# Layer 0 of a gated graph network: the gate's bias as a VectorE add in PSUM in place of a matrix product of ones with its rows

## The chip, the cores and the metric

The kernel runs on one core of one Trainium2 chip. The time is the device time of one execution in microseconds (us), the median of the runs shown. A core has TensorE (PE in the rows; PEld is its loading of weights, the stationary operand, which overlaps the products), VectorE (DVE), ScalarE (ACT), GpSimd (POOL) and the queue that issues the transfers (SP). Each engine works through its own instructions in order and waits for others by semaphores.

## The reference, cut to what matters

The input `x` is 128 graphs of 128 nodes with 256 features, `adj` one 128x128 matrix for each graph. Layer 0 is

```
norm  = (sum(adj, -1) + 1e-6) ** -0.5
f_hom = (adj @ ((x @ theta) * norm)) * norm
f_het = x @ W_h
gate  = sigmoid(x @ W_t + b_t)
x     = layernorm(x + elu(gate * f_hom + (1 - gate) * f_het))
```

Layer 1 (a convolution along the nodes, done by way of spectra, a message product and a gated recurrent cell) follows on the result. The change concerns only how `b_t` gets into `gate`.

## The kernel before

The program has four phases, one after the other: `phase_a` (layer 0, and beside it the spectra of layer 1's filter taps), `phase_spectrum`, `phase_product` and `phase_c`. The change touches `phase_a` alone.

**The tiles.** `phase_a` takes two graphs at a time: 64 pairs. Every product is done at nearly full precision by splitting both operands into a high and a low part (`xh`, `xl`, `w_hi`, `w_lo`) and adding three products (low by high, high by low, high by high), for each of the two halves of the 256 features. So `x @ [theta, W_h]` is 6 products of 512 columns for each graph, into `ps_hh` (line 594), and `x @ W_t` 6 products of 256 columns for each graph, 12 for the pair, into the one PSUM bank `ps_g` (line 640). Ahead of these 12 stands one more product, of a 128x128 tile of ones with `bt_rows` (line 637, 512 columns), which puts the bias in all rows of both halves of `ps_g`. In `bt_rows` row 0 holds the high part of the bias, row 1 the low part, and the others are zero; ScalarE and VectorE make it once, in `more_constants` (lines 302 and 448 to 452).

**The order.** It is written by hand. A step `i` of `step` issues on every engine one stage of several pairs at once: `live(s)` says whether pair `i - s` exists. All 64 + 8 steps are written out, with no loop at run time, and a step looks alike on each engine (numbers are lines):

- TensorE: degrees (603, 604), `x @ [theta, W_h]` of graph 0 (594), fourth spectrum product (586), `adj @ f` of the pair before (615), first spectrum product, 594 of graph 1, second spectrum product, transposes of a finished pair (631), the gate (637, 640), third spectrum product.
- ScalarE: `below` and `ex`, the two halves of elu (342, 345), copy of the fourth spectrum (324), `xh` (353), `ah` (355), `fh` of graph 0 (316), copy of the first spectrum, in every fourth step `th` (366), `fh` of graph 1 (316), `het` (370), copy of the second, `x1t` (377), tanh of the gate, in place in `ps_g` (380), copy of the third spectrum.
- VectorE: `sums_eps` of the degrees (504), `y` (508), statistics (512, 517), `diff` (524), `gd` (531), `mix` (534), `fl` of both graphs (540), `x1` (547), `sums_eps` of the variances (553), in every fourth step `tl` (558).

The four spectrum products of a step go through one PSUM bank, `ps_w`: each waits (`s_gw`) until ScalarE has copied the one before it out. That couples the two queues four times in a step. The gate's products may start when VectorE has read the old `ps_g` (`s_gd`); the tanh waits until they are done (`s_gp`):

```
if live(2):
    reached(act, s_gp, p2 + 1)
    nc.scalar.activation(ps_g[:, :, :], ps_g[:, :, :], ACT.Tanh, scale=0.5).then_inc(s_gate, 1)
if ahead(6):
    spectra_out(t - 6, 2)
```

`sigmoid(z)` is used as `0.5 * (tanh(z / 2) + 1)`; `gd` and `mix` apply the rest.

Of the kernel before, what the change touches and what calls it, by code (L numbers as in the profile page):

```python
# [7 lines left out]
F32 = mybir.dt.float32  # L8
F32R = mybir.dt.float32r
ALU = mybir.AluOpType  # L10
ACT = mybir.ActivationFunctionType

P = 128
D = 256
# [16 lines left out]
def reached(eng, sem, count):  # L31

    if isinstance(count, int) and count <= 0:
        return
    eng.wait_ge(sem, count)
# [34 lines left out]
def phase_a(nc, G, x_n, x_t, adj_t, w0, b_t, masks, x1_t, taps, taps_s, dft_w, w_spec, w_c1, bn1, dft_f, keep, s_spec, s_out, first_x, s_x):  # L70
# [16 lines left out]
    with ExitStack() as ctx:  # L87
        def sb(name, shape, dt=F32):
            return ctx.enter_context(nc.sbuf_tensor("a_" + name, shape, dt))

        def sem(name):
            return ctx.enter_context(nc.semaphore("a_" + name))
# [5 lines left out]
        w_hi = sb("w_hi", [P, KD, 3 * D], F32R)  # L98
        w_lo = sb("w_lo", [P, KD, 3 * D], F32R)
        bt_raw = sb("bt_raw", [P, D])  # L100
        bt_hr = sb("bt_hr", [P, D], F32R)
        bt_h = sb("bt_h", [P, D])
        bt_l = sb("bt_l", [P, D])
        bt_rows = sb("bt_rows", [P, 2, D], F32R)
        ones0 = sb("ones0", [P, P])
        ones = sb("ones", [P, P], F32R)
        ident = sb("ident", [P, P])
        mk = sb("mk", [P, 5])
# [54 lines left out]
        ps_g = ctx.enter_context(nc.psum_tensor("a_ps_g", [P, 2, D], F32))  # L163
# [17 lines left out]
        s_root = sem("norm_and_rstd")  # L181
        s_proj = sem("projected")
        s_gp = sem("gate_projected")
        s_fl = sem("f_low")
        s_het = sem("het_copied")
        s_gate = sem("gate_ready")
# [106 lines left out]
        def _(act):  # L293
# [5 lines left out]

            def more_constants():  # L300
                nc.scalar.activation(dw_hi[:, :], dw_raw[:, :], ACT.Copy).then_inc(s_wh, 1)
                nc.scalar.activation(bt_hr[:, :], bt_raw[:, :], ACT.Copy).then_inc(s_wh, 1)

            def step(i, n, k, live):
                u = n % 2
# [70 lines left out]
                    reached(act, s_out[v], (p - v) * 8)  # L376
                    nc.scalar.activation(x1t[:, v], ps_t[:, :, :], ACT.Copy).then_inc(s_x1t, 1)
                if live(2):
                    reached(act, s_gp, p2 + 1)
                    nc.scalar.activation(ps_g[:, :, :], ps_g[:, :, :], ACT.Tanh, scale=0.5).then_inc(s_gate, 1)  # L380
                if ahead(6):
                    spectra_out(t - 6, 2)
# [54 lines left out]
        def _(dve):  # L437
# [3 lines left out]
                nc.vector.tensor_tensor(w_lo[:, :, :], w_raw[:, :, :], w_hi[:, :, :].bitcast(F32), ALU.subtract).then_inc(s_wl, 1)  # L441

            def more_constants():
                dve.wait_ge(s_wh, 4)

                nc.vector.scalar_tensor_tensor(dw[:, :], dw_hi[:, :].bitcast(F32), mk[0:ROWS, 3:4], dw_raw[:, :],
                                               ALU.mult, ALU.add).then_inc(s_wl, 1)
                nc.vector.tensor_tensor(bt_l[:, :], bt_raw[:, :], bt_hr[:, :].bitcast(F32), ALU.subtract).then_inc(s_wl, 1)
                nc.vector.tensor_scalar(bt_h[:, :], bt_hr[:, :].bitcast(F32), mk[:, 0:1], None, ALU.mult).then_inc(s_wl, 1)
                dve.wait_ge(s_wl, 4)  # L450
                for b in range(2):
                    nc.vector.scalar_tensor_tensor(bt_rows[:, b], bt_l[:, :], mk[:, 1:2], bt_h[:, :], ALU.mult, ALU.add).then_inc(s_wl, 1)

            def step(i, n, k, live):
                u = n % 2
# [93 lines left out]
                if live(5):  # L549
                    reached(dve, s_mv, p5 + 1)  # L550

                    reached(dve, s_root, p5 + 3)
                    nc.vector.scalar_tensor_tensor(sums_eps[:, v, 2:4], mv[:, v, :, 1], 1.0, eps[:, :], ALU.mult, ALU.add).then_inc(s_ve, 1)
                if ahead(1) and tn % TB == 1:
                    m = t // TB
                    reached(dve, s_th, m + 1)
                    reached(dve, s_ts, 48 * m)
                    nc.vector.tensor_tensor(tl[:, :], tr[:, :], th[:, :].bitcast(F32), ALU.subtract).then_inc(s_tl, 1)
# [3 lines left out]
        @block.tensor  # L562
        def _(pe):
            pe.wait_ge(s_wl, 1)
            pe.wait_ge(s_wh, 2)
            pe.wait_ge(s_k, 5)

            def step(i, n, k, live):
                u = n % 2
                v = 1 - u  # L570
                t, tn, tk = i + LEAD, (i + LEAD) % UNROLL, (i + LEAD) // UNROLL
                ahead = taps_live(i)
                p2 = i - 2
                terms = [(xx, ww, c) for c in range(KD) for xx, ww in ((xl, w_hi), (xh, w_lo), (xh, w_hi))]

                def spectra(q, c):
                    r = q % RING
                    if c == 0:
                        reached(pe, s_gs[r], 16 * (q // RING + 1))
                    if q == 0 and c == 0:  # L580
                        pe.wait_ge(s_wl, 2)
                    if t == 18 + LEAD and c == 3:

                        pe.wait_ge(s_ch, 1)
                    reached(pe, s_gw, 4 * q + c)
                    nc.tensor.matmul(ps_w[:, 0:GW], gs[:, r, c], dw[:, :], start=True, stop=True).then_inc(s_gm, 1)  # L586

                def project(b):
                    if b == 0:
                        reached(pe, s_xl, p2 + 1)  # L590
                        reached(pe, s_fl, p2 - 1)
                        reached(pe, s_mix, p2 - 1)
                    for o, (xx, ww, c) in enumerate(terms):
                        last = nc.tensor.matmul(ps_hh[:, 2 * u + b, :], xx[:, u, c, b * P:b * P + P], ww[:, c, 0:2 * D],  # L594
                                                start=(o == 0), stop=(o == len(terms) - 1))
                    last.then_inc(s_proj, 1)

                if live(2):
                    reached(pe, s_al, p2 + 1)

                    reached(pe, s_x1t, i - 7)
                    for b in range(2):
                        nc.tensor.matmul(ps_deg[:, b], al[:, u, b], ones[:, 0:2], start=True, stop=False)
                        last = nc.tensor.matmul(ps_deg[:, b], ah[:, u, b], ones[:, 0:2], start=False, stop=True)
                    last.then_inc(s_deg, 1)
                    project(0)
                if ahead(7):
                    spectra(t - 7, 3)
                if live(3):
                    p = i - 3  # L610
                    reached(pe, s_fl, p + 1)
                    reached(pe, s_diff, p)
                    for b in range(2):
                        for o, (aa, ff) in enumerate(((al, fh), (ah, fl), (ah, fh))):
                            last = nc.tensor.matmul(ps_hom[:, b], aa[:, v, b], ff[:, v, b], start=(o == 0), stop=(o == 2))
                    last.then_inc(s_hom, 1)
                if ahead(6):
                    spectra(t - 6, 0)
                if live(2):
                    project(1)  # L620
                if ahead(6):
                    spectra(t - 6, 1)
                if live(7):
                    p = i - 7
                    reached(pe, s_x1, p + 1)
                    reached(pe, s_x1t, p)

                    reached(pe, s_dege, p2 + 1 if live(2) else pairs)
                    for b in range(2):
                        for c in range(KD):  # L630
                            last = nc.tensor.transpose(ps_t[:, c, b * P:b * P + P], x1[:, v, b, c * P:c * P + P], ident[:, :])
                    last.then_inc(s_xp, 1)
                if i == 2:
                    pe.wait_ge(s_wl, 6)
                if live(2):
                    reached(pe, s_gd, p2)
                    nc.tensor.matmul(ps_g.rearrange("p b d -> p (b d)"), ones[:, :], bt_rows.rearrange("p b d -> p (b d)"), start=True, stop=False)
                    for b in range(2):
                        for o, (xx, ww, c) in enumerate(terms):
                            last = nc.tensor.matmul(ps_g[:, b], xx[:, u, c, b * P:b * P + P], ww[:, c, 2 * D:3 * D],  # L640
                                                    start=False, stop=(b == 1 and o == len(terms) - 1))
                    last.then_inc(s_gp, 1)
                if ahead(6):
                    spectra(t - 6, 2)

                if i == 17:

                    pe.wait_ge(s_gw, 4 * (t - 6) + 3)
                    pe.wait_ge(s_cn, 7)
                    nc.tensor.matmul(ps_w[:, 0:D], ones0[:, :], diag[:, 0].rearrange("p c n -> p (c n)"), start=True, stop=True)  # L650
                    nc.tensor.matmul(ps_w[:, D:2 * D], ones0[:, :], diag[:, 1].rearrange("p c n -> p (c n)"), start=True, stop=True).then_inc(s_bc, 1)

            written_out(pairs, STAGES, step, UNROLL, LEAD)


# [1148 lines left out]
```

## Time and profile before

| | |
|---|---|
| median of 3 runs | 1957.12 us (1956.53 to 1961.15) |
| profiled execution | 1959.8 us, its span 1958.0 us |
| TensorE busy over the span | 1883.0 us (96%) |
| VectorE, ScalarE, GpSimd busy | 1430.3 (73%), 1115.5 (57%), 423.3 us (22%) |
| `phase_a`, about | the first 464 us |

Busy time of TensorE counts overlapping products together, and the ends of products are modelled, so that a busy TensorE is not yet one that never waits. A row of a timeline gives the start and the duration of an instruction (xN: N merged); the next one on the same engine may start before the end of the row, since the ends of instructions overlap. What stands in brackets is idle time ahead of it and what ended it; a wait shorter than the overlap has no bracket, and shows only in the distance between starts.

### The profile page before, as it was taken

To read this page: it belongs to the slowest core of one execution; us is meant where nothing else is said; L and a number is where in the kernel's file an instruction comes from. 1 tells how busy PE (TensorE), PEld (TensorE's weight loads), DVE (VectorE), ACT (ScalarE), POOL (GpSimd) and SP (SyncE) were. 2 spreads that over 40 slices of the span, in tenths; PEclk is the share of its full clock that TensorE was granted. 3 is DMA by queue.
4 is the path that set the end of the run, shared out by engine and by line. 5 is a ranking of instruction groups with operands and counts; after the bars stand their busy time and mean duration, and the time that the engine had idled before them with its cause. 6 is when DMAs were issued, how large, how long until landed. Compare 5 with 4: busy or idle time off the path is not lost.

```text
span 1958.0 us, 35045 instructions
## 1 busy us (share of the span) xinstructions
PE 1883.0 (96%) x11046; PEld 1655.8 (85%) x11046; DVE 1430.3 (73%) x2972; ACT 1115.5 (57%) x2063; POOL 423.3 (22%) x378
## 2 busy tenths in 40 slices
PE   7999999996999899949999999999999999999997
PEld 6988999996999799948888888888888888888886
DVE  5888888885666788856777777777777777777774
ACT  6888888884666677734444444444444444444442
POOL 4766766764454100000000000000000000000000
PEclk9999999997999899969999999999999999999998
DMA  6778888875334688852121211212121212121200
GB/s 220 269 270 287 292 293 293 304 249 193 96 102 145 204 287 275 260 171 91 51 93 59 86 65 68 83 51 99 50 100 50 100 50 93 58 87 64 79 33 22
DMA packets 184169, 281.13 MB, mean 144 GB/s; under 512 B 14286, under 2 KB 126644, under 8 KB 179860
## 3 DMA queue, kind: packets, MB, share of 16 engines
q1 hardware_dynamic: 184084, 280.10, 42.3%
q8 instruction: 41, 0.67, 0.1%
q14 instruction: 44, 0.36, 0.1%
HBM read 178.60 MB, written 101.45 MB: 143 GB/s over the span
## 4 chain that ended last, share of the span: by engine, by line
PE 54%; issue 1%; DVE 1%; ACT 0%; DMA 0%; POOL 0%; POOLq 0%; ACTq 0%; SPq 0%; DVEq 0%
PE c_ps_g L1573 40%; PE c_ps_m L1551 5%; PE c_ps_m L1582 2%; PE c_ps_y L1606 1%; PE c_ps_m L1584 1%; PE c_ps_y L1666 1%; PE c_ps_m L1666 1%; PE c_ps_m L1583 1%; PE c_ps_s L1651 0%; PE c_ps_y L1667 0%; PE c_ps_m L1667 0%; DMA c_x<-x_t 0%; PE c_ps_s L1620 0%; PE c_ps_g L1623 0%; DVE c_wi_l L1517 0%
## 5 line engine op out<-in xcount | busy, mean ns | idle before, releaser
L1333 POOL TENSOR_TENSOR c_rstd<-c_var_eps,c_neg_half 128x4 f32<-128x4 f32 x32 | 32.2, 1007 | 1059.5 <-DVE c_var_eps L1473 1059.5
L1251 ACT ACTIVATE c_yo<-c_ps_y,c_shift,c_rstd 128x256 f32<-128x256 f32 x128 | 61.8, 563 | 169.4 <-DVE c_shift L1481 169.4
L1573 PE MATMUL c_ps_g<-c_ch,c_wi_l 128*128 128x512 f32 x384 | 154.5, 402 | 0.0
L1573 PE MATMUL c_ps_g<-c_nh,c_wi_l 128*128 128x512 f32 x384 | 153.3, 399 | 0.0
L1573 PE MATMUL c_ps_g<-c_xh,c_wh_l 128*128 128x512 f32 x384 | 152.3, 397 | 0.0
L1573 PE MATMUL c_ps_g<-c_xl,c_wh_h 128*128 128x512 f32 x384 | 152.1, 396 | 0.0
L1573 PE MATMUL c_ps_g<-c_xh,c_wh_h 128*128 128x512 f32 x384 | 151.7, 395 | 0.0
L1573 PE MATMUL c_ps_g<-c_ch,c_wi_h 128*128 128x512 f32 x384 | 151.7, 395 | 0.0
L1573 PE MATMUL c_ps_g<-c_cl,c_wi_h 128*128 128x512 f32 x384 | 151.6, 395 | 0.0
L1573 PE MATMUL c_ps_g<-c_nl,c_wi_h 128*128 128x512 f32 x384 | 151.2, 394 | 0.0
L1573 PE MATMUL c_ps_g<-c_nh,c_wi_h 128*128 128x512 f32 x384 | 150.9, 393 | 0.0
L934 PE MATMUL m_ps<-m_wh,m_xl 128*128 128x256 f32 (+1 forms) x406 | 131.7, 324 | 6.2 <-DVE m_wl L918 6.2
L934 PE MATMUL m_ps<-m_wl,s_x 128*128 128x256 f32 (+1 forms) x406 | 131.8, 325 | 0.0
L934 PE MATMUL m_ps<-m_wh,s_x 128*128 128x256 f32 (+1 forms) x406 | 131.1, 323 | 0.0
L415 POOL TENSOR_TENSOR a_roots<-a_sums_eps,a_neg_half 128x4 f32<-128x4 f32 (+1 forms) x68 | 91.3, 1343 | 89.2 <-DVE a_sums_eps L504 81.2
L324 ACT ACTIVATE a_spec<-a_ps_w 128x272 f32<-128x272 f32 x256 | 107.0, 418 | 2.3 <-PE a_ps_w L586 1.4
L594 PE MATMUL a_ps_hh<-a_w_hi,a_xl 128*128 128x512 f32 x256 | 107.1, 418 | 0.0
L729 POOL TENSOR_TENSOR s_xl<-s_x,s_xh 128x512 fp32r<-128x512 f32 x64 | 82.5, 1290 | 94.9 <-ACT s_xh L748 94.9
L594 PE MATMUL a_ps_hh<-a_w_hi,a_xh 128*128 128x512 f32 x256 | 101.7, 397 | 0.0
L594 PE MATMUL a_ps_hh<-a_w_lo,a_xh 128*128 128x512 f32 x256 | 100.6, 393 | 0.0
L1402 DVE SCALAR_TENSOR_TENSOR c_work<-c_ps_g,c_bi,c_work 128x512 f32<-128x512 f32 x64 | 48.0, 751 | 71.4 <-PE c_ps_g L1573 71.4
L420 POOL TENSOR_TENSOR a_xl<-a_xt,a_xh 128x512 fp32r<-128x512 f32 x64 | 84.0, 1312 | 64.8 <-ACT a_xh L353 64.8
(219 smaller groups left out, 6143.1 us busy)
## 6 DMA issues: line engine op xcount, KB each, us to landing
w_spec<-a_spec SPq DMA_DIRECT2D x32, 1088.0 KB, 8.0
m_w<-w_spec SPq DMA_DIRECT2D x34, 1024.0 KB, 8.1
a_xt<-in_x_t SPq DMA_DIRECT2D x64, 256.0 KB, 3.4
a_xn<-in_x_n SPq DMA_DIRECT2D x64, 256.0 KB, 5.1
x_t<-a_x1t SPq DMA_DIRECT2D x64, 256.0 KB, 4.8
s_x<-x_t SPq DMA_DIRECT2D x64, 256.0 KB, 2.9
y_spec<-x_spec SPq DMA_DIRECT2D x64, 256.0 KB, 5.5
c_x<-x_t SPq DMA_DIRECT2D x32, 512.0 KB, 3.9
```

Of the source, the lines that this page charges most:

```text
L324: nc.scalar.activation(spec[:, half, :, first:first + 2], ps_w[:, 0:GW].rearrange("p (d j) -> p d j", j=2), ACT.Copy).then_inc(s_gw, 1)
L415: nc.gpsimd.tensor_tensor(roots[:, u, these], sums_eps[:, u, these], neg_half[:, these], ALU.pow).then_inc(s_root, 1)
L420: nc.gpsimd.tensor_tensor(xl[:, v], xt[:, (n - 1) % RING], xh[:, v].bitcast(F32), ALU.subtract).then_inc(s_xl, 1)
L594: last = nc.tensor.matmul(ps_hh[:, 2 * u + b, :], xx[:, u, c, b * P:b * P + P], ww[:, c, 0:2 * D], start=(o == 0), stop=(o == len(terms) - 1))
L729: nc.gpsimd.tensor_tensor(xl[:, (u - 1) % 2], x[:, r], xh[:, (u - 1) % 2].bitcast(F32), ALU.subtract).then_inc(s_xl, 1)
L934: last = nc.tensor.matmul(out.rearrange("p r (q c) -> p r q c", q=CHUNKS), xx[:, v, c, part], ww[:, v, c].rearrange("p q r c -> p r q c")[ ...
L1251: nc.scalar.activation(yo[:, b], ps_y[:, b], ACT.Identity, bias=shift[:, b:b + 1], scale=rstd[:, b:b + 1]).then_inc(s_yo, 1)
L1402: nc.vector.scalar_tensor_tensor(npre[:, :], ps_g[:, IN_BANK[j], :], bi[:, 2, j:j + 1], hn[:, :], ALU.add, ALU.add).then_inc(s_np, 1)
L1551: last = nc.tensor.matmul(out, stationary, moving, start=(n == 0), stop=(n == len(passes) - 1))
L1573: last = nc.tensor.matmul(out, stationary, moving, start=(count == 0), stop=(count == total - 1))
L1582: nc.tensor.matmul(ps_inv[:, b], yh[:, b, cols], di[:, :, :], start=(b % 2 == 0), stop=False)
L1666: nc.tensor.matmul(both, mh[:, b, j * P:j * P + P], ahl[:, b].rearrange("p s n -> p (s n)"), start=True, stop=False)
```

## The change

The tile `bt_rows` and what makes it are gone (one ScalarE and four VectorE instructions at the start), and so is the product of ones with it. The first of the 12 gate products now opens the bank. A new VectorE instruction, at the end of VectorE's step, adds the bias (`bt_raw`, held on all 128 partitions, read once for each half) to `ps_g` in place. It waits for the products, and the tanh waits for it by a new semaphore, `s_gb`.

```
             def more_constants():
                 nc.scalar.activation(dw_hi[:, :], dw_raw[:, :], ACT.Copy).then_inc(s_wh, 1)
-                nc.scalar.activation(bt_hr[:, :], bt_raw[:, :], ACT.Copy).then_inc(s_wh, 1)
...
                 if live(2):
-                    reached(act, s_gp, p2 + 1)
+                    reached(act, s_gb, p2 + 1)
                     nc.scalar.activation(ps_g[:, :, :], ps_g[:, :, :], ACT.Tanh, scale=0.5).then_inc(s_gate, 1)
...
-                nc.vector.tensor_tensor(bt_l[:, :], bt_raw[:, :], bt_hr[:, :].bitcast(F32), ALU.subtract).then_inc(s_wl, 1)
-                nc.vector.tensor_scalar(bt_h[:, :], bt_hr[:, :].bitcast(F32), mk[:, 0:1], None, ALU.mult).then_inc(s_wl, 1)
-                dve.wait_ge(s_wl, 4)
-                for b in range(2):
-                    nc.vector.scalar_tensor_tensor(bt_rows[:, b], bt_l[:, :], mk[:, 1:2], bt_h[:, :], ALU.mult, ALU.add).then_inc(s_wl, 1)
...
                     nc.vector.scalar_tensor_tensor(sums_eps[:, v, 2:4], mv[:, v, :, 1], 1.0, eps[:, :], ALU.mult, ALU.add).then_inc(s_ve, 1)
+                if live(2):
+                    reached(dve, s_gp, p2 + 1)
+                    nc.vector.tensor_tensor(ps_g[:, :, :], ps_g[:, :, :], bt_raw.rearrange("p (o d) -> p o d", o=1).to_broadcast([P, 2, D]),
+                                            ALU.add).then_inc(s_gb, 1)
...
-                if i == 2:
-                    pe.wait_ge(s_wl, 6)
                 if live(2):
                     reached(pe, s_gd, p2)
-                    nc.tensor.matmul(ps_g.rearrange("p b d -> p (b d)"), ones[:, :], bt_rows.rearrange("p b d -> p (b d)"), start=True, stop=False)
                     for b in range(2):
                         for o, (xx, ww, c) in enumerate(terms):
                             last = nc.tensor.matmul(ps_g[:, b], xx[:, u, c, b * P:b * P + P], ww[:, c, 2 * D:3 * D],
-                                                    start=False, stop=(b == 1 and o == len(terms) - 1))
+                                                    start=(b == 0 and o == 0), stop=(b == 1 and o == len(terms) - 1))
                     last.then_inc(s_gp, 1)
```

On VectorE, the rows of one full step before the change (`a_x` is the layer's result `x1`, `a_ps_t` the bank in which the degrees are summed):

```order
L531 SCALAR_TENSOR_TENSOR a_gd<-a_ps_g,a_diff 128x512
L534 SCALAR_TENSOR_TENSOR a_mix<-a_gd,a_ps_hh 128x512
L540 SCALAR_TENSOR_TENSOR a_fl<-a_ps_hh,a_roots,a_fh 128x256 x2
L547 TENSOR_SCALAR a_x<-a_y,a_mv,a_roots 128x256 x2
L553 SCALAR_TENSOR_TENSOR a_sums_eps<-a_mv,a_eps 128x2
L504 TENSOR_SCALAR a_sums_eps<-a_ps_t 128x2
L508 SCALAR_TENSOR_TENSOR a_y<-a_mix,a_res 128x512
```

The same place in the changed kernel, whose line numbers are a little lower:

```order
L522 SCALAR_TENSOR_TENSOR a_gd<-a_ps_g,a_diff 128x512
L525 SCALAR_TENSOR_TENSOR a_mix<-a_gd,a_ps_hh 128x512
L531 SCALAR_TENSOR_TENSOR a_fl<-a_ps_hh,a_roots,a_fh 128x256 x2
L538 TENSOR_SCALAR a_x<-a_y,a_mv,a_roots 128x256 x2
L544 SCALAR_TENSOR_TENSOR a_sums_eps<-a_mv,a_eps 128x2
L547 TENSOR_TENSOR a_ps_g<-a_ps_g,a_bt_raw 128x512
L495 TENSOR_SCALAR a_sums_eps<-a_ps_t 128x2
L499 SCALAR_TENSOR_TENSOR a_y<-a_mix,a_res 128x512
```

The add stands behind `mix`, `fl`, `x1` and the small `sums_eps`, and ahead of the next step's `sums_eps` of the degrees and of `y`.

On TensorE, the start of the gate in a full step before the change:

```order
L586 MATMUL a_ps_w<-a_dw,a_gs 128x272
L631 MATMUL a_ps_t<-a_ident,a_x 128x128 x4
L637 MATMUL a_ps_g<-a_bt_rows,a_ones 128x512
L640 MATMUL a_ps_g<-a_w_hi,a_xl 128x256
L640 MATMUL a_ps_g<-a_w_lo,a_xh 128x256
```

And in the changed kernel:

```order
L581 MATMUL a_ps_w<-a_dw,a_gs 128x272
L626 MATMUL a_ps_t<-a_ident,a_x 128x128 x4
L632 MATMUL a_ps_g<-a_w_hi,a_xl 128x256
L632 MATMUL a_ps_g<-a_w_lo,a_xh 128x256
L632 MATMUL a_ps_g<-a_w_hi,a_xh 128x256
```

One product in each of 64 steps is gone; nothing else moved there.

## Rows read from the trace of the kernel before

**Rows 1.** Busy time by stretch, 200 to 440 us: five engines, granted clock, transfers.

```profile
core 0: us, PE busy (x) PEld busy (x) DVE busy (x) ACT busy (x) POOL busy (x), PEclk, DMA share, GB/s
200.00:440.00 240.00, 240.00 (x1548) 217.69 (x1547) 206.44 (x548) 207.94 (x476) 167.15 (x145) 1.00 0.83 285
```

**Rows 2.** Timeline of ScalarE in one step, 303 to 308 us: start, duration, instruction.

```profile
303.00 0.47 ACT L316 ACTIVATE a_fh<-a_ps_hh,a_roots 128x256 fp32r<-128x256 f32 x1 [0.48 <-PE a_ps_hh L594]
303.38 0.59 ACT L370 ACTIVATE a_het<-a_ps_hh 128x512 f32<-128x512 f32 x1
...
305.24 0.58 ACT L380 ACTIVATE a_ps_g<-a_ps_g 128x512 f32<-128x512 f32 x1 [0.49 <-PE a_ps_g L640]
305.73 0.43 ACT L324 ACTIVATE a_spec<-a_ps_w 128x272 f32<-128x272 f32 x1
306.02 0.63 ACT L342 ACTIVATE a_below<-a_mix 128x512 f32<-128x512 f32 x1
306.69 0.63 ACT L345 ACTIVATE a_ex<-a_below 128x512 f32<-128x512 f32 x1
307.33 0.41 ACT L324 ACTIVATE a_spec<-a_ps_w 128x272 f32<-128x272 f32 x1
```

**Rows 3.** Timeline of TensorE, the same step.

```profile
301.19 0.36 PE L586 MATMUL a_ps_w<-a_dw,a_gs 102*128 102x272 f32 x1
...
303.29 0.48 PE L637 MATMUL a_ps_g<-a_bt_rows,a_ones 128*128 128x512 f32 x1
303.61 0.28 PE L640 MATMUL a_ps_g<-a_w_hi,a_xl 128*128 128x256 f32 x1
...
304.92 0.28 PE L640 MATMUL a_ps_g<-a_w_hi,a_xh 128*128 128x256 f32 x1
...
307.74 0.28 PE L615 MATMUL a_ps_hom<-a_fh,a_ah 128*128 128x256 f32 x1
307.89 0.36 PE L586 MATMUL a_ps_w<-a_dw,a_gs 102*128 102x272 f32 x1
```

**Rows 4.** The weight load ahead of that last spectrum product.

```profile
307.86 0.19 PEld L586 LDWEIGHTS a_ps_w<-a_dw,a_gs 102*128 102x128 f32 x1
```

**Rows 5.** Timeline of VectorE, the same step.

```profile
301.42 0.88 DVE L524 SCALAR_TENSOR_TENSOR a_diff<-a_ps_hom,a_roots,a_het 128x256 f32<-128x256 f32 x2 [0.42 <-issue]
...
303.24 0.69 DVE L534 SCALAR_TENSOR_TENSOR a_mix<-a_gd,a_ps_hh 128x512 f32<-128x512 f32 x1
304.00 0.88 DVE L540 SCALAR_TENSOR_TENSOR a_fl<-a_ps_hh,a_roots,a_fh 128x256 fp32r<-128x256 f32 x2
304.79 0.73 DVE L547 TENSOR_SCALAR a_x<-a_y,a_mv,a_roots 128x256 f32<-128x256 f32 x2
305.44 0.15 DVE L553 SCALAR_TENSOR_TENSOR a_sums_eps<-a_mv,a_eps 128x2 f32<-128x2 f32 x1
305.71 0.16 DVE L504 TENSOR_SCALAR a_sums_eps<-a_ps_t 128x2 f32<-128x2 f32 x1
305.80 0.69 DVE L508 SCALAR_TENSOR_TENSOR a_y<-a_mix,a_res 128x512 f32<-128x512 f32 x1
```

**Rows 6.** Timeline of VectorE, an early step.

```profile
33.78 0.87 DVE L540 SCALAR_TENSOR_TENSOR a_fl<-a_ps_hh,a_roots,a_fh 128x256 fp32r<-128x256 f32 x2 [0.16 <-ACT a_het L370]
```

**Rows 7.** Timeline of ScalarE: the first and the last of 64 tanh.

```profile
21.80 0.58 ACT L380 ACTIVATE a_ps_g<-a_ps_g 128x512 f32<-128x512 f32 x1 [0.52 <-PE a_ps_g L640]
...
445.44 0.58 ACT L380 ACTIVATE a_ps_g<-a_ps_g 128x512 f32<-128x512 f32 x1 [0.48 <-PE a_ps_g L640]
```

**Rows 8.** Groups of VectorE in `phase_c`: a PSUM operand of 512 columns.

```profile
L1402 DVE SCALAR_TENSOR_TENSOR c_work<-c_ps_g,c_bi,c_work 128x512 f32<-128x512 f32 x64 | 48.0, 751 | 71.4 <-PE c_ps_g L1573 71.4
...
L1427 DVE TENSOR_TENSOR c_mpre<-c_ps_m,c_bm_row 128x512 f32<-128x512 f32 x64 | 43.6, 682 | 0.0
```

**Rows 9.** Timeline of VectorE at the start: the rows that make the bias's tile.

```profile
13.11 0.41 DVE L448 TENSOR_TENSOR a_bt_l<-a_bt_raw,a_bt_hr 128x256 f32<-128x256 f32 x1
...
15.09 0.72 DVE L558 TENSOR_TENSOR a_tl<-a_tr,a_th 128x544 fp32r<-128x544 f32 x1
```

**Rows 10.** Timeline of TensorE at the start, with its clock not yet up.

```profile
14.25 0.35 PE L603 MATMUL a_ps_t<-a_ones,a_al 128*128 128x2 f32 x1 [14.25 <-DVE a_bt_h L449]
...
16.10 0.63 PE L594 MATMUL a_ps_hh<-a_w_hi,a_xh 128*128 128x512 f32 x1
16.53 0.63 PE L594 MATMUL a_ps_hh<-a_w_hi,a_xl 128*128 128x512 f32 x1
```

More of the change, by code:

```diff
@@ L100, in phase_a @@
         bt_raw = sb("bt_raw", [P, D])
[L101 to L104, printed above, removed]
         ones0 = sb("ones0", [P, P])
@@ L183, in phase_a @@
         s_gp = sem("gate_projected")
+        s_gb = sem("gate_biased")
         s_fl = sem("f_low")
@@ L443, in more_constants @@
             def more_constants():
-                dve.wait_ge(s_wh, 4)
+                dve.wait_ge(s_wh, 3)
                 nc.vector.scalar_tensor_tensor(dw[:, :], dw_hi[:, :].bitcast(F32), mk[0:ROWS, 3:4], dw_raw[:, :],
                                                ALU.mult, ALU.add).then_inc(s_wl, 1)
-                nc.vector.tensor_tensor(bt_l[:, :], bt_raw[:, :], bt_hr[:, :].bitcast(F32), ALU.subtract).then_inc(s_wl, 1)
-                nc.vector.tensor_scalar(bt_h[:, :], bt_hr[:, :].bitcast(F32), mk[:, 0:1], None, ALU.mult).then_inc(s_wl, 1)
-                dve.wait_ge(s_wl, 4)
-                for b in range(2):
-                    nc.vector.scalar_tensor_tensor(bt_rows[:, b], bt_l[:, :], mk[:, 1:2], bt_h[:, :], ALU.mult, ALU.add).then_inc(s_wl, 1)
             def step(i, n, k, live):
```

## The prediction

> **What bounds the kernel now.** I read first the busy time by stretch, then the timelines of the engines through one step of layer 0. The table of stretches shows TensorE busy for all of the 240 us from 200 to 440, at the full granted clock, with VectorE at 206.44/240 = 86% and ScalarE at 87% [rows 1]. By that alone TensorE is the bound and a product taken off it is a gain. Busy time hides short waits, though, so the starts have to be compared.
>
> A step repeats every 307.89 - 301.19 = 6.70 us: that is the distance of two "first" spectrum products, here called S [rows 3]. Follow what releases the second one. Its bank, `ps_w`, is freed by ScalarE's copy that starts at 307.33 and ends at 307.74 [rows 2]. The weight load of S starts at 307.86, 0.12 us after that end [rows 4], and S itself follows only 0.03 us behind its load. The product before it started at 307.74 and lasts 0.12 us in the pipeline (the distance in which the products of that kind follow each other: from 303.61 to 304.92 are 11 distances, 0.119 each), so TensorE alone would have been ready at 307.86. S starts at 307.89. So TensorE has at most 0.03 us to spare ahead of S, and ScalarE's copy has none.
>
> What comes before that copy on ScalarE runs without a gap: tanh 305.24, copy of the third spectrum 305.73, `below` 306.02, `ex` 306.69, copy 307.33 [rows 2]. From the start of the tanh to S are 307.89 - 305.24 = 2.65 us, and the reader is to see that each row starts where the one before lets it. The tanh waited 0.49 us for the gate's products [rows 2]; their last one ends at 304.92 + 0.28 = 305.20 [rows 3]. So a closed loop sets the step: S, graph 1's products, transposes, gate, tanh, four more instructions of ScalarE, S. It is 4.05 us from S to the tanh and 2.65 from the tanh to S. TensorE is full, and the loop through ScalarE is just as long. **Whatever makes the tanh later makes the step longer, in full.**
>
> **The change, part by part.**
>
> *The product taken away.* It costs TensorE the distance from its start to that of the first gate product, 303.61 - 303.29 = 0.32 us [rows 3]. Of this some 0.10 is the pick-up after the transposes, which the first gate product will now have (0.32 less the 0.23 at which 512 columns should run; 256 run in 0.12). So 0.22 to 0.32 us are gained, and I take 0.23: the gate's products end at S + 4.01 - 0.23 = S + 3.78.
>
> *The add: when can it start?* It is queued behind `mix`, `fl`, `x1` and the small `sums_eps`. Count from S = 301.19. `fh` of graph 1 starts at +1.81, when TensorE has finished its products (a wait of 0.48 is shown), `het` at +2.19 and ends at 303.97, +2.78 [rows 2]. `fl` starts at 304.00, +2.81, 0.03 us later. It needs `het`, and that it really waits there and not only for `mix` an early step shows: 0.16 us idle, released by `het` [rows 6]. Then `x1` at 304.79, and `sums_eps` at 305.44, +4.25 [rows 5]. A row that follows such a small one starts 0.09 us after it (305.71 to 305.80), so the add may start at +4.25 + 0.07 to 0.09, or, if it should wait for the end of the small one, at +4.40 to 4.45. I take +4.32. The products are done by +3.78: the add waits for VectorE's own queue, not for TensorE. So the 0.23 us that TensorE gained buy nothing.
>
> *The add: how long?* No row of before has VectorE writing PSUM. The nearest ones read 512 columns from PSUM: 0.682 us for the same operation with a row operand, 0.751 for the dearest three-operand form [rows 8]; `mix` 0.69 [rows 5]. I take 0.69, bounds 0.68 and 0.75. Sum: the add ends at +5.01, the tanh follows after a semaphore's 0.03 to 0.10 us (the gaps above), so at S + 5.06, where before it stood at S + 4.05. The trace thus gives a step of 5.06 + 2.65 = 7.71 us in place of 6.70, **1.01 us more**. Low end: 0.68 and the shortest hand-over, 7.67; high end: start at +4.45, 0.75, 0.10 of hand-over, 7.95.
>
> The Trainium skill ("VectorE: DVE Perf Modes", the section on the TRN2 errata) gives a VectorE instruction with PSUM input 120 cycles plus one for each column at 0.96 GHz; for 512 columns that is 0.658 us, an estimate from that page, below the 0.682 us of the rows, and the step by it would be 7.68 us. The measured rows decide, and the difference is 2 us in the whole.
>
> *Does anything else then bind?* With a step of 7.71 VectorE's own work is 6.70 less its 0.42 idle ahead of `diff` and 0.18 ahead of the degrees' `sums_eps` (305.44 to 305.71 where 0.09 would do), so 6.10, plus 0.62 to 0.69 for the add, plus 0.64/4 for `tl` in every fourth step: 6.9 to 7.0 [rows 5], under 7.71. The instructions queued behind the add are `sums_eps` of the degrees and `y`. They start at S + 5.0 in place of 4.52 and 4.61; for the first GpSimd waits, and for it the next `fh`; these are due more than 2 us later, since S itself is late by 1.01. So `gd` is still ready before the gate needs it, and no second loss follows.
>
> *How many steps.* There are 64 tanh, 63 distances, from 21.80 to 445.44 us: 423.64, of which 63 x 6.70 = 422.1 are regular [rows 7]. The first steps, until `x1` is in the loop, have no `x1` ahead of the add: there the add starts when the gate's products end, and the tanh is later by 0.69 + 0.1 - 0.23 = 0.56 us at most. I count 58 distances at 1.01 to 1.03 (6.68 to 6.70 before), 59.2 us, and 2.7 for the first gate and the five distances behind it: 61.9. Against this: VectorE's start is 15.09 - 13.11 = 1.98 us shorter [rows 9], but TensorE was at work from 14.25 with products of 0.43 us distance [rows 10], so it can win between 0 and 1.98, and I take 0.4; and one of the few longer steps (the remaining 1.5 us) may hide in the new slack, 0.5. Sum: **+61 us**. The span of 1958.0 becomes 2019, the profiled execution's 1959.8 becomes 2020.8; it lies 2.7 above the median, and on the median 1957.12 + 61 = **2018 us**. The phases behind layer 0 are not touched and start later by the same amount.
>
> **The rivals.**
>
> *A, the add starts when the products end (7 in 100).* If `fl` or `x1` did not hold it, it would start at S + 3.8 and the tanh at S + 4.61: a step of 7.26, +0.56 x 63 = +35, 1992 us. For it speaks that `mix` alone would release `fl` at the same 304.00 in the step shown; against it, the early row with the wait for `het`, and that `het` hangs on S by rows without slack.
>
> *B, only VectorE's throughput counts (3 in 100).* With 6.9 us of work VectorE would set a step of 6.9 to 7.0: +0.25 x 63 = +16, 1973 us. It holds only if ScalarE's queue had a slack of 0.8 us between tanh and S; the rows show 0.03.
>
> *C, faster (2 in 100).* TensorE is the bound, and the add and the later tanh are hidden: 64 x 0.23 to 0.32 us are saved, 15 to 20 us, 1940 us. The place is the gap between the tanh's `s_gb` and S; it decides from the point where that chain has 1.0 us to spare. TensorE's 100% speak for it [rows 1], the starts against. The Trainium skill ("Perfetto Trace Analysis", Identifying the Most-Contended Engine) says to find the engine with the highest occupancy and to optimize it first, and warns of matmul busy time as a measure; by the first half, this edit is the right one and the time is this rival's 1940. The starts in this trace, with an engine at 100% and a loop through another just as long, do not bear that out.
>
> *D, worse than the sum (11 in 100).* VectorE writing to PSUM costs more than any row, or the longer step meets another wait (the copies of the first spectrum, GpSimd's `al` for the degrees), or TensorE, which now idles some 1 us a step, loses clock. At 8.1 to 8.4 us a step: +85 to +105, 2050 us.
>
> The forecast keeps 77 in 100. Its own range, from 7.60 to 7.95 a step and 0 to 2 us at the start, is 2009 to 2032. The range for 8 in 10 reaches a little to A and D: **2002 to 2035**. A kernel like this can be told from no change at about 0.3%, 6 us. Faster 0.02, same 0.01, slower 0.97.
>
> **What would show it.** In the changed kernel's timelines: tanh to tanh 7.7 us; `het` to `fl` 0.03 us; the add right behind the small `sums_eps` with no idle time released by TensorE; the tanh released by the add; 2.65 us from tanh to S; TensorE idle ahead of S, released by ScalarE's copy, some 0.6 us in each step, and the third spectrum's copy just in time or a little late for the fourth product. An add that waits for the gate's products would be A; a gap on ScalarE between tanh and the copy would be B or C; and if `phase_c` changed its length, something that I have not seen is at work.

## The result and the profile after

The changed kernel takes 2012.96 us (median of 4 runs, 2012.29 to 2016.25) where the kernel before, run beside it, takes 1958.18 (1956.53 to 1961.15): a ratio of 1.0283 with an interval of 1.0266 to 1.0299, 54.8 us slower. Forecast were 61 us and 2018. The profiled execution has a span of 2011.6 us against 1958.0.

Busy time of the stretch from 200 to 440 us after the change, beside [rows 1]:

```profile
core 0: us, PE busy (x) PEld busy (x) DVE busy (x) ACT busy (x) POOL busy (x), PEclk, DMA share, GB/s
200.00:440.00 240.00, 222.63 (x1344) 186.30 (x1344) 199.52 (x518) 181.18 (x424) 148.35 (x128) 1.00 0.78 263
```

No engine is full any more. TensorE lost 17 us of busy time in these 240 and VectorE, which was given work, is less busy too: fewer steps fit. Something between the engines sets the step.

ScalarE in one full step, to be laid beside [rows 2] (S, the "first" spectrum product of the step, starts at 327.73 here):

```profile
329.51 0.47 ACT L312 ACTIVATE a_fh<-a_ps_hh,a_roots 128x256 fp32r<-128x256 f32 x1 [0.44 <-PE a_ps_hh L589]
329.89 0.59 ACT L366 ACTIVATE a_het<-a_ps_hh 128x512 f32<-128x512 f32 x1
...
332.74 0.58 ACT L376 ACTIVATE a_ps_g<-a_ps_g 128x512 f32<-128x512 f32 x1 [1.48 <-DVE a_ps_g L547]
333.24 0.40 ACT L320 ACTIVATE a_spec<-a_ps_w 128x272 f32<-128x272 f32 x1
333.52 0.63 ACT L338 ACTIVATE a_below<-a_mix 128x512 f32<-128x512 f32 x1
334.18 0.63 ACT L341 ACTIVATE a_ex<-a_below 128x512 f32<-128x512 f32 x1
334.72 0.38 ACT L320 ACTIVATE a_spec<-a_ps_w 128x272 f32<-128x272 f32 x1
```

VectorE in that step, beside [rows 5]:

```profile
330.51 0.88 DVE L531 SCALAR_TENSOR_TENSOR a_fl<-a_ps_hh,a_roots,a_fh 128x256 fp32r<-128x256 f32 x2 [0.62 <-ACT a_het L366]
331.31 0.73 DVE L538 TENSOR_SCALAR a_x<-a_y,a_mv,a_roots 128x256 f32<-128x256 f32 x2
331.95 0.15 DVE L544 SCALAR_TENSOR_TENSOR a_sums_eps<-a_mv,a_eps 128x2 f32<-128x2 f32 x1
332.02 0.69 DVE L547 TENSOR_TENSOR a_ps_g<-a_ps_g,a_bt_raw 128x512 f32<-128x512 f32 x1
```

TensorE in it, beside [rows 3]: S, the last gate product, and the next S:

```profile
327.73 0.36 PE L581 MATMUL a_ps_w<-a_dw,a_gs 102*128 102x272 f32 x1 [0.45 <-ACT a_spec L320]
...
331.20 0.28 PE L632 MATMUL a_ps_g<-a_w_hi,a_xh 128*128 128x256 f32 x1
...
335.24 0.37 PE L581 MATMUL a_ps_w<-a_dw,a_gs 102*128 102x272 f32 x1 [0.45 <-ACT a_spec L320]
```

Read round the loop. S starts at 327.73 and `fh` 1.78 us later, then comes `het`. `fl` starts 0.03 us behind the end of `het` and is now named as waiting for it. `x1` and the small row follow. The add starts at S + 4.29, with no idle time ahead of it, although the gate's products had ended at 331.20 + 0.28 = S + 3.75. The tanh starts at S + 5.01 and the next S 2.50 us behind the tanh: 7.51. In the kernel before the tanh stood at S + 4.05.

The waits from 30 to 510 us (us in total, times, the longest) say the same for nearly all of the 64 steps:

```profile
ACT a_ps_g L376 <- DVE a_ps_g L547: 93.5, 63, 2.0
...
DVE a_fl L531 <- ACT a_het L366: 33.9, 61, 1.1
PE a_ps_w L581 <- ACT a_spec L320: 29.6, 62, 2.1
```

And the two groups by line, from 0 to 520 us:

```profile
L547 DVE TENSOR_TENSOR a_ps_g<-a_ps_g,a_bt_raw 128x512 f32<-128x512 f32 x64 | 44.3, 692 | 0.0
...
L376 ACT ACTIVATE a_ps_g<-a_ps_g 128x512 f32<-128x512 f32 x64 | 37.2, 582 | 94.8 <-DVE a_ps_g L547 94.8
```

The add never waited (0.0 behind the bar), and the tanh waited for it 94.8 us in all.

Where the 53.6 us between the spans lie: the tanh run from 23.72 to 498.12 us, 474.40 for 63 distances against 423.64 [rows 7]. Of the 50.8 us, 48.7 fall on the last 58 distances (439.33 against 390.62, 0.84 each, 7.52 for 6.68 in most steps) and 2.05 on the first five. The first tanh is 1.92 us later, and the time from the last tanh to the first product of the next phase grew by 1.3. All that follows keeps its length within 0.4 us.

### The profile page after: what moved, and what is told of

Same layout as the page of the kernel before. It is cut to its first block, busy times and chain, and to the rows that moved or that the text cites. A ratio compares the mean times of both kernels' runs of the same rounds, so it can differ in the third digit from the quotient of the medians.

```text
span 2011.6 us, 34976 instructions
## 1 busy us (share of the span) xinstructions
PE 1900.0 (94%) x10982; PEld 1642.4 (82%) x10982; DVE 1460.9 (73%) x3032; ACT 1106.9 (55%) x2062; POOL 422.9 (21%) x378
## 4 chain that ended last, share of the span: by engine, by line
PE 52%; issue 1%; DVE 1%; ACT 0%; DMA 0%; POOL 0%; POOLq 0%; ACTq 0%; SPq 0%; DVEq 0%
PE c_ps_g L1565 39%; PE c_ps_m L1543 5%; PE c_ps_m L1574 2%; PE c_ps_y L1598 1%; PE c_ps_m L1576 1%; PE c_ps_y L1658 1%; PE c_ps_m L1658 1%; PE c_ps_m L1575 1%; PE c_ps_s L1643 0%; PE c_ps_y L1659 0%; PE c_ps_m L1659 0%; DMA c_x<-x_t 0%; PE c_ps_g L1615 0%; PE c_ps_s L1612 0%; DVE c_wi_l L1509 0%
## 5 line engine op out<-in xcount | busy, mean ns | idle before, releaser
L581 PE MATMUL a_ps_w<-a_dw,a_gs 102*128 102x272 f32 x256 | 85.9, 335 | 36.1 <-ACT a_spec L320 29.6
L581 PEld LDWEIGHTS a_ps_w<-a_dw,a_gs 102*128 102x128 f32 x256 | 48.4, 189 | 78.6 <-issue 38.3
```

## The experiments

Edits are against the changed kernel unless "before" is said. Ratios are to the kernel before. Three points inside a line of a diff stand for operands left out.

**The add further ahead on VectorE** (`e1_add_before_x1`): is it the queue that holds the add?

```diff
                     last.then_inc(s_fl, 1)
+                if live(2):
+                    reached(dve, s_gp, p2 + 1)
+                    nc.vector.tensor_tensor(ps_g..., ps_g..., bt_raw..., ALU.add).then_inc(s_gb, 1)
                 if live(6):
...
-                if live(2):
-                    reached(dve, s_gp, p2 + 1)
-                    nc.vector.tensor_tensor(ps_g..., ps_g..., bt_raw..., ALU.add).then_inc(s_gb, 1)
```

> The add is issued right behind fl, ahead of x1 and the small sums_eps. Loop theory (the step is set by S, fh, het, fl, x1, sums_eps, add, tanh, S): x1 and sums_eps leave the loop, the add then starts at the later of S + 3.6 (fl's slot) and the end of the gate's products, S + 3.75; tanh at S + 4.5, step 7.0 to 7.2 us in place of 7.52, the kernel 1982 to 1995 us, between before and the change. Rival (only VectorE's total work counts): the same instructions, so no change, 2013 us. Rival (the add waits for the products in any case): no change either.

Measured 1985.7 us, ratio 1.0132 (1.0115 to 1.0149), steps of 7.03, and some 7.3 in every fourth. VectorE's and ScalarE's rows of one step:

```profile
301.99 0.88 DVE L531 SCALAR_TENSOR_TENSOR a_fl<-a_ps_hh,a_roots,a_fh 128x256 fp32r<-128x256 f32 x2 [0.30 <-ACT a_het L366]
302.99 0.70 DVE L536 TENSOR_TENSOR a_ps_g<-a_ps_g,a_bt_raw 128x512 f32<-128x512 f32 x1
303.73 0.58 ACT L376 ACTIVATE a_ps_g<-a_ps_g 128x512 f32<-128x512 f32 x1 [0.99 <-DVE a_ps_g L536]
```

Half of the loss is gone with the same work on every engine. The add costs by its place.

**No bias at all** (`e2_no_bias`): the product gone and no add in its place, so the gate's bias is left out. This is what the removed product was worth.

```diff
-                    reached(act, s_gb, p2 + 1)
+                    reached(act, s_gp, p2 + 1)
...
-                if live(2):
-                    reached(dve, s_gp, p2 + 1)
-                    nc.vector.tensor_tensor(ps_g..., ps_g..., bt_raw..., ALU.add).then_inc(s_gb, 1)
```

> Leaves the bias out altogether: no product of ones, no add; the tanh waits for the gate's products as before. Shows what the removed product alone is worth. Loop theory with TensorE full in the kernel before: 0.23 us a step at most, step 6.45 to 6.6 us, 1943 to 1953 us. Rival (the product was hidden behind another loop, TensorE only looked full): 1956 to 1960 us, no change.

Measured 1952.7 us, ratio 0.9970 (0.9960 to 0.9979), steps of 6.57. The product of ones was worth 0.11 us a step, some 6 us in all.

**The add over 2 columns** (`e3_add_2_columns`): order and semaphores stay, the length goes; the bias is added to 2 of 512 columns and left out in the rest.

```diff
-                    nc.vector.tensor_tensor(ps_g[:, :, :], ps_g[:, :, :], bt_raw...to_broadcast([P, 2, D]), ALU.add).then_inc(s_gb, 1)
+                    nc.vector.tensor_tensor(ps_g[:, 0, 0:2], ps_g[:, 0, 0:2], bt_raw[:, 0:2], ALU.add).then_inc(s_gb, 1)
```

> The add at its place, with its waits, but over 2 columns in place of 512, so that the rest of the bias is left out. Loop theory: its start stays at S + 4.25 to 4.3, it lasts 0.15 in place of 0.69, the step is 0.5 us shorter, 6.95 to 7.05 us, 1981 to 1986 us: of the loss some 33 us are the length of the add and the rest its place in the queue. Rival (VectorE's total work): the work falls under the others and the time comes to that without bias, under 1957 us.

Measured 1978.3 us, ratio 1.0102 (1.0085 to 1.0119), steps of 6.99; the time came out 3 us under the expected range, the step inside it. The add and the tanh behind it:

```profile
304.98 0.16 DVE L547 TENSOR_TENSOR a_ps_g<-a_ps_g,a_bt_raw 128x2 f32<-128x2 f32 x1
305.18 0.58 ACT L376 ACTIVATE a_ps_g<-a_ps_g 128x512 f32<-128x512 f32 x1 [0.95 <-DVE a_ps_g L547]
```

An add of almost nothing still costs 20 us. Of the 0.84 us a step, 7.52 - 6.99 = 0.53 is the add's length (0.692 less 0.16), and the rest, 0.31, is that the tanh now hangs on VectorE's queue.

**The same work, with nobody waiting** (`e4_idle_add`): VectorE adds the bias to a tile of its own, and the tanh waits for the products again. The bias is left out of the gate.

```diff
-                    reached(act, s_gb, p2 + 1)
+                    reached(act, s_gp, p2 + 1)
...
-                    reached(dve, s_gp, p2 + 1)
-                    nc.vector.tensor_tensor(ps_g..., ps_g..., bt_raw..., ALU.add).then_inc(s_gb, 1)
+                    reached(dve, s_gb, p2 + 1)
+                    nc.vector.tensor_tensor(scrap[:, :, :], scrap[:, :, :], bt_raw..., ALU.add).then_inc(s_gb, 1)
```

> No bias, and at the add's place an add of the same size on a tile of its own, for which nobody waits. Shows the price of VectorE's extra work by itself. Loop theory: VectorE's work of 6.85 to 6.95 us a step becomes the longest, 1963 to 1975 us, much under the change's 2013: most of the loss is the wait of the tanh. Rival (VectorE's total work sets the changed kernel): 2013 us. If VectorE had room it would come to the kernel with no bias.

Measured 1960.6 us, ratio 1.0011 (1.0001 to 1.0020), 2 us below the range. Most steps are 6.4 to 6.6, and 7.12 in every fourth, where `tl` stands on VectorE as well. So the bare load on VectorE costs some 8 us over the kernel without a bias, where the waited-for add costs 60 over the same kernel.

**The tanh later in ScalarE's queue** (`f10_tanh_after_ex`): the add stays where the change put it, the tanh moves behind the next step's `ex`.

```diff
                     nc.scalar.activation(ex[:, :, :], below[:, :, :], ACT.Exp, scale=-1.0).then_inc(s_ex, 1)
+                if live(3):
+                    reached(act, s_gb, i - 2)
+                    nc.scalar.activation(ps_g..., ps_g..., ACT.Tanh, scale=0.5).then_inc(s_gate, 1)
...
-                if live(2):
-                    reached(act, s_gb, p2 + 1)
-                    nc.scalar.activation(ps_g..., ps_g..., ACT.Tanh, scale=0.5).then_inc(s_gate, 1)
```

> The changed kernel with its tanh moved on ScalarE: behind the next step's below and ex, ahead of the copy of the fourth spectrum. The third spectrum's copy, below and ex no longer wait for the add. Loop theory: c2 at about S + 3.9, ex done at S + 5.4, tanh at about S + 5.5 (add done by S + 5.0), copy at S + 6.0 behind the fourth product at S + 5.8: the loop is 6.5 to 6.6 us, and VectorE's work is what is left, 6.7 to 6.9 us a step, as with the idle add: 1957 to 1972 us, near the kernel before. Rival (the loss is VectorE's writing to PSUM, or the add's length in any place): it stays above 2000 us. Rival (gd now waits for the tanh): 1980 us and more, with idle time ahead of gd released by the tanh.

Measured 1959.1 us, ratio 1.0006 (0.9997 to 1.0015), most steps 6.4 to 6.6 and 7.1 in every fourth, as with the idle add: the whole loss is gone. ScalarE in one step, and the add:

```profile
308.32 0.62 ACT L338 ACTIVATE a_below<-a_mix 128x512 f32<-128x512 f32 x1
308.97 0.64 ACT L341 ACTIVATE a_ex<-a_below 128x512 f32<-128x512 f32 x1
309.51 0.58 ACT L344 ACTIVATE a_ps_g<-a_ps_g 128x512 f32<-128x512 f32 x1
310.03 0.40 ACT L320 ACTIVATE a_spec<-a_ps_w 128x272 f32<-128x272 f32 x1
...
308.32 0.69 DVE L547 TENSOR_TENSOR a_ps_g<-a_ps_g,a_bt_raw 128x512 f32<-128x512 f32 x1
```

The tanh has no wait left, because `below` and `ex` do their 1.2 us ahead of it while VectorE adds (its add ran from 308.32 to 309.01). The copy that frees the bank for S follows the tanh directly.

**The control of that move** (`g3_before_tanh_after_ex`): the same edit in the kernel before.

> The kernel before, product of ones kept, with the tanh moved on ScalarE behind ex as in the run with the moved tanh. A control. Loop theory: before, TensorE's own queue set the step, so freeing the copies from the tanh gives nothing: 1953 to 1961 us, the same as before. Rival (the tanh's place was a bound before as well, and the moved tanh only pays the add with a gain of its own): faster by as much as the add's work costs, 1945 to 1952 us.

Measured 1959.7 us, ratio 1.0001 (0.9992 to 1.0011). The move is worth nothing by itself, so the tanh's place did not set the step before; after the change the move takes the add out of the loop.

**The fourth spectrum's copy ahead of `ex`** (`f6_copy_before_ex`): the other way to shorten the stretch from the tanh to S.

```diff
+                if ahead(7):
+                    spectra_out(t - 7, 3)
...
                     nc.scalar.activation(ex[:, :, :], below[:, :, :], ACT.Exp, scale=-1.0).then_inc(s_ex, 1)
-                if ahead(7):
-                    spectra_out(t - 7, 3)
```

> The changed kernel with ex and the copy of the fourth spectrum swapped on ScalarE: one instruction less between the tanh and S. In the changed kernel ex stands for 0.54 us there. Loop theory: the loop loses up to 0.54 us, a step of 7.0 if nothing else is late, up to 7.4 since ex, xh, ah and with them GpSimd's res and al are no earlier: 1981 to 2005 us, in any case under 2013. Rival (S waits for something else than this copy): 2013 us.

Measured 2003.6 us, ratio 1.0224 (1.0209 to 1.0240), steps of 7.32 and 7.46: a gain of 9 us, at the weak end of what was expected. The stretch from tanh to S shrank from 2.50 to 1.93 us (tanh at 319.62, S at 321.55), and the step by only 0.06 to 0.20. From that S to the next tanh, though, are 5.38 us where they were 5.01, and the difference is `x1`. In the changed kernel it started at 331.31 and GpSimd's `al` ended at 331.42; here it runs into `al`:

```profile
325.00 0.74 POOL L430 TENSOR_TENSOR a_al<-a_at,a_ah 128x256 fp32r<-128x256 f32 x1
325.13 1.09 DVE L540 TENSOR_SCALAR a_x<-a_y,a_mv,a_roots 128x256 f32<-128x256 f32 x2
```

The pair took 1.0 us or more in 44 of 64 steps, where it takes 0.73 in the changed kernel. The last section has more on this. What holds the steps of 7.46 was not followed.

**`tl` on GpSimd** (`f11_tanh_after_ex_tl_on_pool` on top of the late tanh, `f12_before_tl_on_pool` in the kernel before): to take the long fourth step away.

```diff
+                if taps_live(i)(1) and tn % TB == 1:
...
+                    nc.gpsimd.tensor_tensor(tl[:, :], tr[:, :], th[:, :].bitcast(F32), ALU.subtract).then_inc(s_tl, 1)
...
-                    nc.vector.tensor_tensor(tl[:, :], tr[:, :], th[:, :].bitcast(F32), ALU.subtract).then_inc(s_tl, 1)
```

> As with the moved tanh, and the tl subtraction of every fourth step on GpSimd, behind al, in place of VectorE. Every fourth step of the idle-add kernel took 7.12 us in place of 6.5, those with tl. Loop theory with VectorE's work as the bound: these steps come down by 0.3 to 0.6 us, 16 of them, 5 to 9 us less than with the moved tanh alone: 1950 to 1965 us, at or a little below the kernel before. Rival (GpSimd, which feeds xl and al, becomes late): no better than the moved tanh alone, with TensorE waiting for al.

> The kernel before with tl on GpSimd, as a control for the run ahead of this one. TensorE sets its step and VectorE has 0.6 us to spare, so within 3 us of the kernel before, 1955 to 1961 us. If it came out faster, the gain of the other would not be the add's.

Both missed. The first took 1964.7 us, ratio 1.0037 (1.0025 to 1.0050): just inside its wide range, but 5.6 more than without the move where 5 to 9 less were expected. The control took 1963.4, ratio 1.0025 (1.0016 to 1.0034), 4.8 more than the kernel before where no more than 3 were expected. The last section tells the likely reason.

**The start kept** (`g1_start_kept`): the change with the five instructions that made the bias's tile put back with their waits, unused.

```diff
+                nc.scalar.activation(bt_hr[:, :], bt_raw[:, :], ACT.Copy).then_inc(s_wh, 1)
...
+                nc.vector.tensor_tensor(bt_l..., bt_raw..., bt_hr..., ALU.subtract).then_inc(s_wl, 1)
...
+                    nc.vector.scalar_tensor_tensor(bt_rows[:, b], bt_l..., mk[:, 1:2], bt_h..., ALU.mult, ALU.add).then_inc(s_wl, 1)
```

> The changed kernel with the five instructions that made the bias's tile kept at the start, so that only the product and the add differ from before. In the changed kernel TensorE starts 0.38 us later than before and reaches its full clock some 2 us later. If the missing instructions are the cause (VectorE's tl then runs beside GpSimd's al), TensorE starts at 14.25 again, and the first tanh comes at 22.3 to 22.7 us in place of 23.72; the whole 1.0 to 1.5 us shorter. If the clock's rise differs from run to run, first product to full clock is 4.6 or 6.6 us here as it pleases. Steps of 7.52 us either way.

Measured 2012.7 us (2 runs), ratio 1.0271 (1.0250 to 1.0291), the first tanh at 23.39 and the first product at 14.61. The whole is 0.3 us shorter than the changed kernel, not 1.0 to 1.5, and the first tanh and the first product came later than expected. The changed kernel once more, with nothing edited (`g2_after_again`), had its first tanh at 22.72 and a span of 2008.9:

> The changed kernel once more, to see whether its late full clock at the start repeats: 6.6 us after the first product, as in its first profile, or 4.6, as in the kernel before.

So 1.0 us of the first tanh's delay comes and goes without any edit. The rest of the 2.7 us between the two spans lies behind layer 0's last tanh (498.12 and 498.57).

## Why the prediction was right, step by step

**That the tanh is in the loop that sets the step:** right. The late tanh (1959.1) removes the loss while every engine does the same work, and the idle add (1960.6) shows what that work costs without the wait.

**Why TensorE's relief buys nothing:** right in the changed kernel. The gate's products end 0.3 us earlier and the add starts 0.5 us behind their end. Without the add the relief would have been worth 0.11 us a step, and not the 0.23 taken from TensorE. The rows show where the other 0.13 goes. The degrees' first product takes `al` as its weights. Here it is in `e2_no_bias`, and under it in the kernel before, each behind the `al` that it needs:

```profile
300.13 0.75 POOL L428 TENSOR_TENSOR a_al<-a_at,a_ah 128x256 fp32r<-128x256 f32 x1
300.94 0.27 PE L594 MATMUL a_ps_t<-a_ones,a_al 128*128 128x2 f32 x1
```

```profile
304.12 0.76 POOL L432 TENSOR_TENSOR a_al<-a_at,a_ah 128x256 fp32r<-128x256 f32 x1
305.17 0.17 PE L603 MATMUL a_ps_t<-a_ones,a_al 128*128 128x2 f32 x1
```

Without the bias it starts 0.05 or 0.06 us behind the end of `al`, in each of the 36 steps from 200 to 440 us; in the kernel before it was 0.24 to 0.29 behind. From the third spectrum product to the first product of `x @ [theta, W_h]` TensorE then needs 0.62 us where it needed 0.49. So by these distances the next to hold TensorE is GpSimd; no run separates it.

**The add's start and length:** S + 4.32 forecast, S + 4.29 found; 0.69 us forecast, 692 ns found over 64; tanh at S + 5.06 forecast, 5.01 found. Every row that was to show the mechanism does, two of them at another size: 2.50 us from tanh to S for 2.65, and 0.45 us of idle time on TensorE ahead of S for 0.6. Rival A would have shown an add waiting for the products: the group has 0.0 us of that. B (1973) and C (1940) needed slack between the tanh and S; there was little. VectorE's throughput alone, B's price, was put at 16 us; the idle add puts it at 2 over the kernel before, 8 over the one without a bias, and the late tanh, whose add does work in PSUM, at 1 and 6. Nothing of D showed: the PSUM write took 692 ns, and the granted clock from 200 to 440 us stayed at 1.00.

**The step that was mis-sized: from the tanh to S, 2.65 us taken, 2.50 found.** The prediction said that there "each row starts where the one before lets it". One did not. Here is TensorE's fourth spectrum product in the kernel before, in the step of [rows 3]:

```profile
307.00 0.29 PE L586 MATMUL a_ps_w<-a_dw,a_gs 102*128 102x272 f32 x1
```

It ends at 307.29, and the copy at 307.33 [rows 2] reads the bank that it writes. Behind `ex` at 306.69 that copy came 0.64 us later. After the change the product had long been done:

```profile
333.69 0.39 PE L581 MATMUL a_ps_w<-a_dw,a_gs 102*128 102x272 f32 x1
```

There the copy comes 334.72 - 334.18 = 0.54 us behind `ex`. Over the steps from 100 to 440 us the medians say the same: before, the copy starts 0.04 us behind the end of the product and 0.65 behind `ex`; after, 0.64 and 0.54. So in the kernel before the copy waited for TensorE and not for the tanh, and there were 0.10 to 0.15 us of slack between tanh and S, which the later tanh used up first. The trace named no releaser, since the wait was shorter than the overlap of two instructions on ScalarE. With the 0.05 us by which the tanh came sooner than forecast, the step is 0.84 us longer in place of 1.01, and 58 x 0.17 = 10 us less in all.

**The start:** the first tanh came 1.92 us later, where the prediction had 0.4 us less for VectorE's shorter start and at most 0.56 more for the first add. This offset part of the error above, by luck. The 1.92 has three parts.

0.38 us is the first product, at 14.63 and not at 14.25 [rows 10]. It did not wait for the bias's rows, though the row of before names one. It starts 0.14 or 0.15 us behind the end of GpSimd's `al` in the kernel before, in the changed kernel and with the start kept, in this order:

```profile
12.85 1.25 POOL L432 TENSOR_TENSOR a_al<-a_at,a_ah 128x256 fp32r<-128x256 f32 x1
```

```profile
12.93 1.56 POOL L428 TENSOR_TENSOR a_al<-a_at,a_ah 128x256 fp32r<-128x256 f32 x1
```

```profile
13.20 1.26 POOL L433 TENSOR_TENSOR a_al<-a_at,a_ah 128x256 fp32r<-128x256 f32 x1
```

So VectorE's shorter start had nothing to give. It even cost 0.31 us: without the bias's rows VectorE does `tl` earlier, beside `al`, and `al` takes longer. With the start kept `al` is short again. That its first product still comes at 14.61 is because the whole chain began 0.35 us later in that execution: from the start of `w_lo` on VectorE (10.01, 10.08 and 10.36) the first product comes after 4.24, 4.55 and 4.25 us.

0.87 us is the add. The last of the gate's first products starts at 22.53, and at 21.48 before; the tanh stood 0.32 us behind it and now stands 1.19 behind, because the first add is queued behind `fl` (22.21) and does not start when the products end:

```profile
22.53 0.28 PE L632 MATMUL a_ps_g<-a_w_hi,a_xh 128*128 128x256 f32 x1
23.00 0.69 DVE L547 TENSOR_TENSOR a_ps_g<-a_ps_g,a_bt_raw 128x512 f32<-128x512 f32 x1
```

The remaining 0.67 us is how long TensorE's products stay 0.43 us apart, less the product taken away; that differs between executions (below).

Summed: the 58 steps brought 48.7 us where 59.2 less 0.5 was forecast, 10.0 less. The first tanh and the first five distances are 1.92 + 2.05 = 3.97 us where 2.7 less 0.4 was forecast, 1.7 more, and the end of the phase is 1.3 that was not forecast. That is 54.0, against 53.6 in the spans.

## What to carry to other kernels

An engine at 100% is not the bound by that alone: count from start to start round each loop through the in-order queues, and ask of each row which engine let it start, since a wait shorter than the overlap of two instructions leaves no mark. Moving work off the full engine loses when the new place is the last of a queue on which the loop then waits; with the product gone, the same add cost 55 us at the end of the queue, 27 us ahead of `x1` and the small row, and 1 us once the consumer had other work to do first. When a hand-over between two engines is added, look at the consumer's queue for instructions that need nothing from it, and let them go first.

## What the runs showed that was not expected

**VectorE's `x1` waits for a subtraction that runs on GpSimd.** In `f12_before_tl_on_pool`, VectorE's `x1` in a step without `tl` and in one with it:

```profile
307.73 0.73 DVE L553 TENSOR_SCALAR a_x<-a_y,a_mv,a_roots 128x256 f32<-128x256 f32 x2
...
314.41 1.91 DVE L553 TENSOR_SCALAR a_x<-a_y,a_mv,a_roots 128x256 f32<-128x256 f32 x2
```

GpSimd at that moment:

```profile
314.49 1.36 POOL L438 TENSOR_TENSOR a_tl<-a_tr,a_th 128x544 fp32r<-128x544 f32 x1
```

The pair of `x1` takes 1.91 us for 0.73 and ends at 316.32. A narrower window shows that it is the first of the two that is held:

```profile
314.41 1.58 DVE L553 TENSOR_SCALAR a_x<-a_y,a_mv,a_roots 128x256 f32<-128x256 f32 x1
```

It ends at 315.99, 0.14 us behind GpSimd's end at 314.49 + 1.36 = 315.85. In the changed kernel's step at 331.31 it takes 0.40 us. In `f6_copy_before_ex` the same is seen with `al`: the first `x1` takes 0.77 us, from 325.13 to 325.90, and `al` ends at 325.74. In `f12_before_tl_on_pool` it is 1.2 us in nearly every fourth step, more than the 0.64 that VectorE saved by handing `tl` over. It is the only delay of that size seen in those steps, and so the likely reason why both moves lost; a run that separates it was not made. The Trainium skill ("SBUF — State Buffer", the section "Who interferes with whom") says that a tensor_scalar in its two-port mode and GpSimd exclude each other for a whole instruction, and that the one which issues first holds the ports. The trace agrees with the whole instruction's wait. Whether `x1` runs in that mode, and who had issued first, its rows don't show: in one run `x1` starts 0.08 us ahead of GpSimd's instruction, in the other 0.13 behind it, and it waits in both.

**VectorE adds in place in PSUM nearly as fast as it reads from there:** 692 ns for 512 columns, with 0.60 us from its start to that of the next instruction, against 682 with the result in SBUF [rows 8].

**TensorE's slow products at the start last differently long in executions of one kernel.** In the changed kernel the products were still 0.43 us apart at 20.55 us; in its repetition they were 0.22 to 0.24 apart from 18.85:

```profile
20.12 0.63 PE L589 MATMUL a_ps_hh<-a_w_lo,a_xh 128*128 128x512 f32 x1
20.55 0.63 PE L589 MATMUL a_ps_hh<-a_w_hi,a_xh 128*128 128x512 f32 x1
```

```profile
18.85 0.40 PE L589 MATMUL a_ps_hh<-a_w_lo,a_xh 128*128 128x512 f32 x1
19.09 0.39 PE L589 MATMUL a_ps_hh<-a_w_hi,a_xh 128*128 128x512 f32 x1
```

The first product starts at 14.63 and at 14.70. The granted clock of the profile reads 1.00 in both from 16 to 20 us and so doesn't tell the two apart. What decides it stays open; between these two executions it moved the first tanh by 1.0 us.
